# Negated maxima of the attention: their matmuls eight slots later, their turns and the routing's counts further behind what they read

## The reference

```
x = x + mixer(layernorm(x))             # state-space mixer: 64 heads, chunks of 128 tokens
x = x + attention(layernorm(x), ctx, ctx)
x = x + experts(layernorm(x))           # 8 experts, each token goes to its best 2

attention: q = 32 heads of 16; k = v = ctx as 8 heads of 16 (4 query heads share one)
  scores = q k^T / sqrt(16);  attn = softmax(scores);  out = attn v
experts: logits = rmsnorm(x) * router_scale @ router_logits -> two largest per token
  out = sum over the two of weight * (gelu(x Wg) * (x Wu)) Wd
```

## Time and profile before

| | |
|---|---|
| Median of 3 runs | 1454.18 us (1453.34 to 1455.5) |
| The profiled execution's own time | 1459.7 us |
| Its span | 1457.9 us |
| Busy: PE, DVE, ACT, POOL | 1343.5, 877.1, 723.6, 586.2 us |
| Mean granted PE clock | 0.954 of 2.4 GHz |

### The profile page before, as it was taken

One profiled execution on the slowest core, in us unless ns is written; L12 is line 12 of the kernel. 1 busy time (PEld: TensorE's weight loads), 2 busy tenths in 40 slices (PEclk: granted clock), 3 DMA queues, 4 the chain that ended last, 5 costly groups with the idle time before them and its releaser, 6 DMA issues.

```text
span 1457.9 us, 23107 instructions
## 1 busy us (share of the span) xinstructions
PE 1343.5 (92%) x7729; PEld 734.2 (50%) x7729; DVE 877.1 (60%) x1838; ACT 723.6 (50%) x1390; POOL 586.2 (40%) x871
## 2 busy tenths in 40 slices
PE   6699999999999999998888888888999999999997
PEld 4456566666666665654333433323444444444443
DVE  5797898979797979757888888855111111111111
ACT  2676667667666676663576776762111111111110
POOL 1365465555455465675223245243222222222221
PEclk9899999999999999997898997988999999999999
DMA  9000000000000000000211110002443354244322
GB/s 338 10 8 5 8 5 1 12 1 12 1 8 5 8 6 8 13 1 5 97 34 34 34 34 31 30 30 74 121 134 114 66 138 135 46 130 132 58 44 29
DMA packets 40291, 73.00 MB, mean 50 GB/s; under 512 B 18544, under 2 KB 22896, under 8 KB 39152
## 3 DMA queue, kind: packets, MB, share of 16 engines
q1 hardware_dynamic: 30240, 48.10, 9.5%
q0 software_dynamic: 8736, 20.61, 7.6%
q10 hardware_dynamic: 1200, 2.82, 0.5%
HBM read 148.91 MB, written 19.99 MB: 116 GB/s over the span
## 4 chain that ended last, share of the span: by engine, by line
PE 68%; DVE 21%; issue 5%; ACT 3%; POOL 2%; DMA 1%; SPq 1%; POOLq 0%; DVEq 0%; ACTq 0%
PE work_ps L539 12%; PE gate_ps L1530 9%; PE up_ps L1530 9%; PE down_ps L1514 9%; PE work_ps L611 7%; DVE conv L820 7%; PE work_ps L544 4%; DVE maxes L1220 3%; PE work_ps L633 3%; PE work_ps L1046 3%; PE mturn_ps L544 2%; PE decay_ps L1037 2%; DVE mix L736 2%; PE decay_ps L621 2%; PE work_ps L1022 1%
## 5 line engine op out<-in xcount | busy, mean ns | idle before, releaser
L539 PE MATMUL work_ps<-xnT,w_in 128*128 128x256 f32 (+1 forms) x1216 | 299.8, 391 | 2.8 <-DVE xdt L860 2.1
L736 POOL TENSOR_TENSOR mix<-decay,cbm 128x512 f32<-128x512 f32 x128 | 182.9, 1431 | 221.6 <-ACT decay L731 190.6
L539 PEld LDWEIGHTS work_ps<-xnT,w_in 128*128 128x128 f32 (+1 forms) x1216 | 219.2, 188 | 65.1 <-issue 33.4
L727 ACT ACTIVATE decay<-decay_ps 128x512 f32<-128x512 f32 x256 | 154.3, 603 | 111.6 <-PE decay_ps L621 111.0
L1618 POOL DMA_INDIRECT out_dram<-y_out,ids x39 | 61.9, 1587 | 334.3 <-DVE row_w L1582 228.9
L1220 DVE TENSOR_REDUCE maxes<-work_ps 128x2 f32<-128x512 f32 x256 | 166.6, 683 | 33.7 <-PE work_ps L1022 32.1
L820 DVE SCALAR_TENSOR_TENSOR conv<-raw,conv_w,conv 128x256 f32<-128x256 f32 x240 | 177.7, 746 | 6.6 <-ACT conv L687 0.7
L1118 ACT ACTIVATE prob<-decay_ps 128x512 f32<-128x512 f32 x256 | 142.2, 609 | 75.3 <-PE decay_ps L1037 74.4
L1597 DVE TENSOR_TENSOR act<-gelu,up_ps 128x512 f32<-128x512 f32 x39 | 26.8, 688 | 252.1 <-PE up_ps L1530 252.1
L731 ACT ACTIVATE decay<-decay 128x512 f32<-128x512 f32 x256 | 163.9, 640 | 4.7 <-PE work_ps L539 3.0
L1530 PE MATMUL gate_ps<-w_e,xgT 128*128 x312 | 140.5, 593 | 1.4 <-ACT xgT L1547 1.0
(11 more groups left out here) (270 smaller groups left out, 1975.8 us busy)
## 6 DMA issues: line engine op xcount, KB each, us to landing
w_e<-c_experts_dram SPq DMA_DIRECT2D x39, 3072.0 KB
normed_tokens<-r_xn SPq DMA_DIRECT2D x17, 256.0 KB, 2.1
out_dram<-x_sb SPq DMA_DIRECT2D x17, 256.0 KB, 2.5
x_sb<-x_dram SPq DMA_DIRECT2D x1, 3072.0 KB, 16.8
w_in<-c_w_inT_dram ACTq DMA_DIRECT2D x1, 2560.0 KB, 12.7
w_in<-c_w_inT_dram SPq DMA_DIRECT2D x1, 2048.0 KB, 9.1
w_out<-c_w_outT_dram SPq DMA_DIRECT2D x1, 2048.0 KB, 21.9
RT<-cum_scratch SPq DMA_DIRECT2D x32, 48.0 KB
```

Source lines behind the costliest of these rows:

```text
L539: m = e.matmul(ps[0:width, at:at + L], w_in[:, k, col:col + width], xnT[b % 2][:, k, :], start=(k == 0), stop=(k == KD - 1))
L727: e.activation(decay[s % 5][:, :], decay_ps[s % 3][:, :], ACT.Relu, scale=-1.0).then_inc(piece_done[stage], 1)
L736: return e.tensor_tensor(four(mix[s % 5]), four(decay[s % 5]), cb, ALU.mult)
```

## The change

`LEAD` goes from 5 to -3: `max(b, p)` stands at slot `n*(b-1) + p + 3`, which is slot 3 of the batch before to slot 2 of its own. `nmax` follows (slots 12 and 28 of the batch before become 20 and 4 of its own). `n_turn` goes from one slot behind `nmax` to four, `n_copy` and `n_out` from two to five. `c_count` and what follows it in groups 0 and 1 stand four slots later. The preparation of batch 1 stands five slots later, `place` of tiles 8 to 11 at other slots, and `among` gives the slots -40 to -25 the five mixer slots that -40 to -33 had. No instruction is added or removed.

```diff
-LEAD = 5
+LEAD = -3
...
     for b in range(NB):
-        r = n * (b - 2)
+        r = n * (b - 2) + (5 if b == 1 else 0)
...
             put(n * (b - 1) + n // 2 * (h + 1) - LEAD + 1, ("nmax", b, h))
-            put(n * (b - 1) + n // 2 * (h + 1) - LEAD + 2, ("n_turn", b, h))
-            put(n * (b - 1) + n // 2 * (h + 1) - LEAD + 3, ("n_copy", b, h), ("n_out", b, h))
+            put(n * (b - 1) + n // 2 * (h + 1) - LEAD + 5, ("n_turn", b, h))
+            put(n * (b - 1) + n // 2 * (h + 1) - LEAD + 6, ("n_copy", b, h), ("n_out", b, h))
...
         put(at, ("c_scale", g), ("c_newton", g))
-        put(at + 3, ("c_rank", g), ("c_count", g))
-        put(at + 5, ("c_logit", g), ("c_exp", g))
-        put(at + 6, ("c_slots", g))
+        apart = 4 if g < 2 else 0
+        put(at + 3, ("c_rank", g))
+        put(at + 3 + apart, ("c_count", g))
+        put(at + 5 + apart, ("c_logit", g), ("c_exp", g))
+        put(at + 6 + apart, ("c_slots", g))
         if g < 2:
-            put(at + 9, ("c_weight", g), ("c_weight_out", g))
+            put(at + 9 + apart, ("c_weight", g), ("c_weight_out", g))
     for t in range(12):
         for c in range(2):
-            put(n * 5 + 4 * t if t < 8 else n * 7 + 8 + 4 * (t - 8) + 2 * c, ("place", c, t))
+            put(n * 5 + 4 * t if t < 8 else n * 7 + 12 + 3 * (t - 8) + 2 * c, ("place", c, t))
...
-        for at, end, first, width in ((-54, -40, NS_STEPS - 20, 9), (-40, -33, NS_STEPS - 11, 4.9), (-33, -1, NS_STEPS - 3, 19)):
+        for at, end, first, width in ((-54, -40, NS_STEPS - 20, 9), (-40, -25, NS_STEPS - 11, 4.9), (-25, -1, NS_STEPS - 3, 19)):
```

## The result

The changed kernel takes 1468.16 us (median of 4 runs, 1466.79 to 1475.41) against 1454.1 for the kernel before on the same chip: ratio 1.0106, interval 1.0071 to 1.014. It is slower by about 1.1%, where the forecast was 1449.2 us and the range ended at 1458. Its profiled execution took 1469.11 us, with a span of 1467.3, 9.4 more than before. In the changed kernel the lines named here have numbers two higher than before (L1028 is now L1030), and in experiment 9 one higher still.

The account below looks back on a forecast made before the run. Attention was taken as bound in turn by DVE, something serial, then PE. Terms -2.0 (turns), -3.1 and +0.1 (maxima), others 0, gave -5.0 us: median 1454.18 to 1449.2 us; forecast's own range 1446 to 1452, overall 1441 to 1458.

Parts of the forecast that it names:

- After slot 17 PE is full, and all it gains there is clock. I change nothing for it: PE behind `r_turn`: the gap moves but does not vanish, so no clock change was priced, 0 us.
- part 2: `c_count` four slots behind `c_rank`: PE would stand at a bank instead, DVE sets the time; 0, bounds 0 and 3.5 us.
- Turns (-2.0 us): `n_turn` four slots behind `nmax`: PE waits at the product's bank, then `r_turn`; slack there returns 2.0 of 9.3 us.
- everything only moves: Rival: product's bank and `r_xn` take the turn's whole wait, POOL holds the mixer's end; -0.5, 1453.7 us, chance 0.20.
- The rival that gave the clock a price: Slower rival: moved gap at `r_turn` drops the clock where PE is full; +6.5 us, 1460.7 us, chance 0.13.
- Maxima arriving (+0.1): Eight maxima arriving in slots 219 to 226: scores there cost PE +0.1 us for all eight, at most 0.4.
- Maxima leaving (-3.1): Eight earliest maxima leaving the mixer's last units before slot 0: 0.39 us each, -3.1 us, bounds 0 and 5.4.
- Transfers: `n_out` transfer of the turned maxima, 7 slots ahead of its score: needs 5.0 us, has 5.9 to 6.6, so covered.
- The ring order: On the DMA queue: the small transfer starts only behind the expert weights, about 716 rather than 713 us, still covered.
- The sign I had named: Attention window, 702 to 974 us: prediction wrong if the granted clock leaves 0.88 by more than 0.02.

Follow-up runs that it names:

- experiment 9: Changed kernel with only group 1's `c_exp` three slots later, `c_logit` left beside `attend`: ratio 1.0026, 1459.33 us.
- experiment 3: Kernel before with only the counts part: count, `c_logit`, `c_exp`, `c_slots` of groups 0 and 1 four slots later, `place` moved: ratio 1.0033, 1461.58 us.
- experiment 6: Kernel before, nothing moved, with five filler matmuls in front of `n_turn` of half 0 in batches 2 to 7: ratio 0.9985, 1454.24 us.
- experiment 2: Kernel before with only the turns of the maxima later (`n_turn` four slots behind `nmax`, `n_copy` and `n_out` five), LEAD still 5: ratio 1.006, 1463.5 us.
- experiment 1: Changed kernel with group 1's count, `c_logit`, `c_exp` and `c_slots` put back, group 0 still four slots later: ratio 1.0087, 1469.03 us.
- experiment 4: Changed kernel with everything of the routing groups put back (counts, logits, `c_slots`, `place`), maxima and turns still changed: ratio 1.0049, 1464.18 us.
- experiment 8: Changed kernel with group 1's `c_logit` and `c_exp` put back from slot 233 to 229, count left late: ratio 1.011, 1473.13 us.
- experiment 10: Kernel before with only the turns of the maxima later, plus six filler matmuls in front of the sixth batch's `r_turn`: ratio 0.998, 1453.66 us.
- experiment 12: Changed kernel with group 1's `c_exp` three slots later and six filler matmuls in front of the sixth batch's `r_turn` alone: ratio 0.9986, 1458.04 us.
- experiment 11: Changed kernel with six filler matmuls before `r_turn` in batches 0 to 5, and group 1's `c_logit` and `c_exp` back at slot 229: ratio 1.0054, 1464.34 us.

## Why the prediction was wrong, point by point

Two steps of the sum failed, both of them terms put at nothing. The first is "After slot 17 PE is full, and all it gains there is clock. I change nothing for it": the clock behind the sixth batch's `r_turn` cost 7.4 us in the profile. The second is the **0** of part 2, which looked at the counts of group 0 only: `c_exp` of group 1, moved along with them, led to 8.6 us in the profile. The sum of -5.0 us had neither.

**Turns (-2.0 us).** The steps were seen rightly: the turn's wait gone, then a wait at the product's bank of over 1 us (1.5 to 1.9), then one at `r_turn`. At slot 209 POOL's last step ends at 931.47 and PE starts at 932.47, at the floor of 1.0 us. The value was wrong: over the first 208 slots the sum came to 0.0 us, the counts of group 0 included. For this stretch that is the rival "everything only moves".

**The clock at `r_turn` (0 in the sum).** The reason for the 0 was that the gap only moves. The rival that gave the clock a price was wrong in its sizes: it "decides from about three batches of six on", with 5.1 us beyond `r_turn` in each. One batch decided. In the first five, PE's waits at `r_turn` were 0.3, 1.0, 0.4, 1.2 and 1.0 us; in the sixth 2.67, and its slow stretch was 13.6 us long, not 5.1. The window between scores 208 and 216 grew by 7.4 us. I had read 0.82 us at that `r_turn` as evidence against this rival. It was the rest of a longer gap: the turn ahead of it had waited 1.29 us, and PE's work between the two had been stretched by the slow clock. At full clock the rest was 2.33 us (experiments 3 and 6). With the turn gone, one wait of 2.67 us is left. The rival's kind was right, and its chance of 0.13 far too low. That its 1460.7 comes near experiment 2 (1.006) is luck: it added up six batches of 5.1 us, and a gain of 3.1 us from the maxima that experiment 2 doesn't have.

**Counts (0).** The case of group 0 went as told: 3.46 us at the count became 3.55 us at a bank. But I priced only that group. Of group 1 I looked at the count and not at what moves along with it: `c_exp` in ACT's queue, `c_logit` beside `attend` in slot 232. "What of it lies beside other work" was asked of POOL's load alone (101 of 272 us), not of what DVE does during `attend`. The row for it was in the trace of before, in a step that nobody waits for:

```profile
959.95 0.83 DVE L1330 TENSOR_TENSOR weight<-weight,mean_sq 128x32 f32<-128x32 f32 x1
960.81 1.20 DVE L1331 TENSOR_TENSOR weight<-weight,e_scale 128x32 f32<-128x32 f32 x1
```

None of the rivals names this place. The stretch grew by 8.6 us in the profile, and moving `c_exp` alone (experiment 9) took 0.8% off.

**Maxima arriving (+0.1).** As PE's price that held: from score 216 to 232 it lost 0.5 us. It left out DVE, where eight folds of 0.68 us, 5.4 us in all, now stand ahead of group 1's rank. Experiments 1, 4 and 8 each ran into them: 3.54 us of PE at the count, or 2.94 us of ACT at `c_exp`; experiment 3, without them, had neither. The counts and the logits can't simply be put back.

**Maxima leaving (-3.1).** The first score came 7.6 us earlier in the profile, and 3.1 was too little, but 7.6 is too much. From one and the same mixer unit (at 599.3 us before) to the first score, the four experiments with the maxima in front (2, 3, 6 and 10) have 99.9 to 100.6 us in their traces, and eight of the nine kernels with the maxima behind 95.2 to 96.4 (the ninth 99.6); the profile of before had 103.5 and is the odd one out. About 4 us is the price of the move, close to the term.

**Transfers.** No score waited for a DMA, as said. SP issued the weights at 699.35, 7 us earlier than I had put it, and the small transfer behind them:

```profile
699.35 0.43 SPq L1459 DMA_DIRECT2D w_e<-c_experts_dram  x1
705.79 1.33 SPq L1465 DMA_DIRECT2D qT<-nmaxT  x2
709.54 0.38 SPq L1452 DMA_DIRECT2D xbc<-ctx_dram  x1
```

SP's next issue, behind its landing, came 3.75 us after it, where 3.1 had been measured before; its reader was at 712.60. The DMA engines were full until about 708 us, so the landing is some 1.4 us behind the weights. The ring order that the prediction cited from the Trainium skill (page "DMA: Bandwidth & Descriptors", section "Queues, rings and completion order") fits that, though one transfer doesn't show it. It was covered.

**The sign I had named.** I wrote that the prediction is wrong if the clock of 702 to 974 leaves 0.88 by more than 0.02. It is 0.87, and the prediction is wrong all the same. A mean over 272 us hides 14 us at half the clock, the fault that I had found with means in my own first paragraph. The window also ends at 974, 14.5 us ahead of the last score of the changed kernel (988.48).

**What stays open.** Waits of 1.75 to 2.69 us ahead of the full stretch at slot 209 were followed by 13.6 us at 1.2 GHz in six of the eight traces that have one there, and by 6.8 us, in two pieces, in two (experiments 1 and 3). What makes the difference isn't settled. Nor was LEAD's part tried without the later turns; only turns alone and counts alone were. With the turns and the counts back in their old places the changed LEAD has no valid order, as maximum 19 of batch 2 would need a bank whose fold (18) stands behind it in the list, so that kernel never ran. And fillers in front of `r_turn` on top of the kernel before, with nothing moved, weren't run. Experiment 3 suggests that the kernel before can lose time at that place too. So a part of what the fillers gave in experiments 10 and 12 may be a gain over the kernel before, and not the change's loss mended.

## What to carry to other kernels

Before a wait is moved, add up the idle time that stands ahead of the next gate on the same engine: waits of 1.3 and 0.8 us, with slowed work between them, become one of 2.7 us, and if PE is full behind it, the clock can cost several times the wait. When a group of pieces is moved, walk through each of its instructions on each in-order queue, also those of the second group, and ask what stands behind it: here one activation of 0.23 us stood at the head of ACT's queue and held the exponents for 3 us. And once a gap that costs clock is found, fillers on PE are a test that separates the clock from the wait, as in experiments 2 and 10.

## What the runs showed of the hardware

Some small DVE steps that read SBUF, beside an instruction of POOL, end only when that instruction ends. POOL's two `attend` instructions of 1.27 us start at 958.93; DVE's L1302 starts at 958.96 and ends at 960.22, L1303 starts at 960.25 and ends at 961.46; the same steps took 0.17 and 0.19 us elsewhere. The rows of L1330 and L1331 above are two more cases, in the kernel before. Not every step is held: a fold, which reads PSUM, took its usual 0.68 us at 782.60 while `attend` ran from 781.51 to 783.98, and a reciprocal with one SBUF input took 0.18 us at 959.73 beside the `attend` of 959.46. The Trainium skill, page "GPSIMD Engine Reference", section "8. Key points", says that POOL shares its SBUF interfaces with DVE and contends with DVE instructions with two SBUF inputs or in a 2-port mode. The traces fit that as to L1303, L1330 and L1331, which have two inputs by their rows; no row shows in which mode L1302 ran. In all four the step lasts until POOL's instruction is through.

The clock's answer to a wait is uneven. In the changed kernel the 2.67 us were followed by 13.6 us at 1.2 GHz, while the fourth batch's `r_turn`, at 856.25 behind a wait of 1.23 us, lies in 16 us at full clock:

```profile
850.00:866.00 16.00, 13.12 (x122) 6.97 (x120) 13.67 (x40) 10.84 (x20) 6.83 (x29) 1.00 0.22 75
```

With the same 2.94 us on ACT and 1.59 on PE, experiment 8's trace fell to 1.2 GHz for 17 us and experiment 11's didn't fall. The spread of one kernel's times goes along with it: on the chip of experiment 12 the kernel before took 1453.18 us at a mean clock of 0.958 and 1466.26 us at 0.949. That the uneven answer makes this spread isn't shown apart.
